# Running the value products of two key chunks one after the other, with seven score buffers

## The reference

```
q = (norm(x) @ wq.T + bq)      # 8 batches x 128 queries x 512
k = (ctx @ wk.T + bk)          # 8 batches x 2048 keys x 512
v = (ctx @ wv.T + bv)
scores = einsum('bhqd,bhkd->bhqk', q, k) / sqrt(32)      # 16 heads of 32
attn = softmax(scores)
out = einsum('bhqk,bhkd->bhqd', attn, v) @ wo.T + bo
```

## Time and profile before

| | |
|---|---|
| median of 3 runs | 1833.36 us (1832.06 to 1834.14) |
| the profiled execution, its own time | 1831.57 us |
| its span | 1829.8 us |
| granted TensorE clock, mean | 0.977 |
| TensorE busy | 1710.6 us, 93% of the span |
| VectorE busy | 1200.3 us, 66% |
| ScalarE busy | 962.1 us, 53% |
| GpSimd busy | 695.6 us, 38% |

### The profile page before, as it was taken

The page is one execution under the profiler, slowest core; times in us unless marked ns, Lnnn a source line. Parts: engine busy times, 40 slices in busy tenths (PEclk is TensorE's granted clock), DMA queues, the critical chain, the costliest instruction groups (busy, mean ns, idle before and its releaser), DMA issues. The chain is left out here.

```text
span 1829.8 us, 37829 instructions
## 1 busy us (share of the span) xinstructions
PE 1710.6 (93%) x15768; PEld 1376.8 (75%) x15768; DVE 1200.3 (66%) x1631; ACT 962.1 (53%) x1470; POOL 695.6 (38%) x315
## 2 busy tenths in 40 slices
PE   6899999999999999999999998567999689979999
PEld 5688888888888888888888887566887466658886
DVE  5126887878778778778778787767323677753223
ACT  2236666666666666666666666653210678730000
POOL 0003555555555555555555554002001466622220
PEclk9999999999999999999999999789999899999999
DMA  4211111111011011011110101042560533101101
GB/s 162 73 47 38 32 35 41 27 39 41 27 39 42 27 39 42 28 39 37 32 39 30 39 16 63 16 132 109 179 184 2 161 91 103 58 25 46 49 19 46
DMA packets 104192, 105.00 MB, mean 57 GB/s; under 512 B 7263, under 2 KB 72799, under 8 KB 104044
## 3 DMA queue, kind: packets, MB, share of 16 engines
q1 hardware_dynamic: 104044, 102.83, 18.5%
HBM read 79.74 MB, written 23.07 MB: 56 GB/s over the span
## 5 line engine op out<-in xcount | busy, mean ns | idle before, releaser
L528 POOL TENSOR_TENSOR b_acc<-b_acc,b_s 128x1024 f32<-128x1024 f32 x168 | 458.6, 2730 | 268.5 <-ACT b_s L731 258.1
L793 DVE TENSOR_TENSOR b_mx<-b_psS,b_mx 128x512 f32<-128x512 f32 x480 | 331.3, 690 | 50.0 <-PE b_psS L600 36.9
L760 DVE TENSOR_TENSOR b_s<-b_s,b_mb 128x2048 f32<-128x2048 f32 x128 | 350.9, 2743 | 15.7 <-ACT b_mb L718 15.7
L731 ACT ACTIVATE b_s<-b_s 128x2048 f32<-128x2048 f32 x128 | 245.1, 1915 | 67.1 <-DVE b_s L760 67.1
L740 ACT ACTIVATE b_s<-b_psS 128x2048 f32<-128x2048 f32 x128 | 241.1, 1883 | 56.3 <-DVE b_mx L793 55.9
L43 PE MATMUL b_work<-cT,wkT 128*128 128x512 f32 x512 | 210.7, 412 | 0.0
L43 PE MATMUL b_work<-wvT,cT 128*128 128x512 f32 x512 | 209.4, 409 | 0.0
L44 PE MATMUL b_work<-cT,wkT 128*128 128x512 f32 x512 | 200.8, 392 | 0.0
L45 PE MATMUL b_work<-cT,wkT 128*128 128x512 f32 x512 | 200.5, 392 | 0.0
L45 PE MATMUL b_work<-wvT,cT 128*128 128x512 f32 x512 | 200.2, 391 | 0.0
L44 PE MATMUL b_work<-wvT,cT 128*128 128x512 f32 x512 | 200.0, 391 | 0.0
(11 more groups left out here) (224 smaller groups left out, 3056.7 us busy)
## 6 DMA issues: line engine op xcount, KB each, us to landing
cin<-in_ctx SPq DMA_DIRECT2D x64, 512.0 KB, 3.7
q_scratch<-d_st SPq DMA_DIRECT2D x32, 256.0 KB, 2.5
k_scratch<-d_st SPq DMA_DIRECT2D x32, 256.0 KB, 2.5
e_q<-q_scratch SPq DMA_DIRECT2D x16, 512.0 KB, 3.5
k_sb<-k_scratch SPq DMA_DIRECT2D x64, 128.0 KB, 3.7
experts_sb<-in_L_ffn_expert_w SPq DMA_DIRECT2D x8, 1024.0 KB, 5.3
x_sb<-in_x SPq DMA_DIRECT2D x2, 1024.0 KB, 7.0
q_scratch<-a_q SPq DMA_DIRECT2D x4, 512.0 KB, 3.2
```

What stands on the lines that cost most here:

```text
L528: nc.gpsimd.tensor_tensor(acc[:, :, :], acc[:, :, :], s[:, buf, 2 * i:2 * i + 2, :], ALU.add).then_inc(sum_done, 1)
L731: nc.scalar.activation(part, part, ACT.Exp, scale=SCALE).then_inc(exp_done, 1)
L760: nc.vector.tensor_tensor(s[:, n % BUFS, :, :], s[:, n % BUFS, :, :], mb[:, :].rearrange("p (o n) -> p o n", o=1).broadcast_to([P, CHUNK, ...
L793: nc.vector.tensor_tensor(mx[:, :, :], part, mx[:, :, :], ALU.max).then_inc(mx_done, 1)
```

## The change

The value products of chunks 2k and 2k + 1 now stand in one beat, 34 + 4k, one right after the other. Chunks 0 and 1 stand in beat 2 of eight, chunks 2 and 3 in beat 6, both between T and S; beats 1 and 4 have none. There are seven score buffers in place of six (8 KB more of each partition).

```diff
-        BUFS = 6
+        BUFS = 7
...
-        def value_step(beat):
-
-            early, late = steps(beat, 32, 2, SLOTS * CHUNK), steps(beat, 33, 2, SLOTS * CHUNK)
-            if early is not None and early % CHUNK:
-                return early
-            return late if late is not None and late % CHUNK == 0 else None
+        def value_steps(beat):
+
+            n = steps(beat, 34, 4, SLOTS * CHUNK // 2)
+            return () if n is None else (2 * n, 2 * n + 1)
...
-                if (n := value_step(beat)) is not None:
+                for n in value_steps(beat):
                     outputs(n)
```

## The result

The changed kernel takes 1817.22 us (median of 6 runs, 1815.16 to 1820.62), the kernel before 1833.55 us in its six. The ratio is 0.9908, 95% interval 0.9895 to 0.9922: faster by 0.92%. Forecast were 1818.3 us, 14.5 us less. The medians differ by 16.3 us, and the interval of the ratio stands for 14.3 to 19.3 us. The profiled execution took 1817.25 us with a span of 1815.5, against 1831.57.

The account below looks back on a forecast made before the run. TensorE's instruction order bounds up to beat 255, a VectorE and ScalarE chain the tail. 0.47 us a slot over 28 slots, 13.0 us, plus 1.5 us tail, taken from 1832.8, gives 1818.3 us; 8-in-10 range 1813 to 1826.

Parts of the forecast that it names:

- Chunk 0: Projected region: its value product, alone between two projections, costs 1.20 us, appended 0.873; 0.33 us saved a slot.
- Chunk 2: Projected region: its value product between T and S costs 1.01 us, appended 0.873; 0.14 us saved a slot.
- The appended O: A value product right behind another costs 0.873 us, read from the tail; bounds 0.81 and 1.01 us.
- The prediction's sum by pauses alone: Projected region: two modes fewer entered and left a slot, about 0.2 us each over 28 slots, 11 us.
- The slack of 1.04 us: Between the end of chunk 3's move and S of chunk 0, 7.65 us after S of chunk 3; costed at nothing.
- the forecast break-even: Beat 4: the slot's 0.47 us gain is used up when the move ends over 8.12 us after its S starts.
- The rival: S of chunk 0, beat 4: the score move becomes the bound; at 8.6 us, about 1847 us; chance 0.04.
- The tail: After the projections, where S, maxima and move set the pace: 1.5 us gained, ends -4 and +2.
- The gain behind M: Tail: without O of chunk 2 the maxima start 1.06 us earlier, in two slots, 2.1 us.
- The loss before S of chunk 1: Tail: two pairs with denominators precede this S; they fit at full clock, but end near 3 us late at half clock.
- The rival by which joining saves little: Each O costs 1.01 us joined or not; 4 to 7 us gained with the tail, about 1827 us; chance 0.08.
- The rival by which the tail gives it back: Groups before S of chunk 1 run at half clock both times; 9 us left, about 1824 us; chance 0.12.

Follow-up runs that it names:

- the two partial changes: Against the kernel before, with seven buffers: only chunks 0 and 1 joined, 1823.40 us, ratio 0.9944; only chunks 2 and 3 joined, 1829.09 us, ratio 0.9971.
- the two groups: Tail stretches of profiles: old order of value products 90.43, 90.48, 92.94 us; pairs in the tail 88.80, 88.96, 89.45, 88.61, 89.26 us.

## Why the prediction was right

**What bounds.** TensorE's order set the time of the projected region before and after: the region shrank by what TensorE's own row of instructions lost, and repeats to 0.01 us when it is left alone.

**The terms.** Chunk 0: 0.33 us forecast, 0.36 measured by the experiment that moved it alone. Chunk 2: 0.14 forecast, 0.134 measured. Together 0.464 against 0.494 us a slot, 13.0 against 13.84 us. The missing 0.03 us is in the price of the lone O. The loads of two projections, from the second load behind S to T, first before and then in the changed kernel, where no O stands between them (the T of before is in the earlier trace rows):

```profile
616.85 0.19 PEld L44 LDWEIGHTS b_work<-cT,wkT 128*128 128x128 f32 x1
```

```profile
610.31 0.19 PEld L44 LDWEIGHTS b_work<-cT,wkT 128*128 128x128 f32 x1
...
612.60 0.19 PEld L45 LDWEIGHTS b_work<-cT,wkT 128*128 128x128 f32 x1
...
615.55 0.58 PEld L563 LDWEIGHTS b_work<-ident,cin 128*128 128x128 f32 x4
```

That is 623.32 - 616.85 = 6.47 us against 615.55 - 610.31 = 5.24: the O had cost 1.23 us, not 1.20. I had counted the steps behind the O as if they were the same without it. They take 0.229 us behind the O (eleven steps from 620.80 to 623.32) and 0.227 us deep in a run (thirteen from 612.60 to 615.55).

The appended O costs 0.87 to 0.88 us, as read from O and denominators in the tail; it was the term with the widest bounds and it held. The medians differ by 16.3 us and the two changed stretches of the profiles by 15.5; what is left is within what the unedited stages differ by.

**That it is the change of kind.** The transposes between the pair undo it all with the beats untouched, and the buffer alone is nothing. By the Trainium skill, TensorEngine Tiling (Array Packing), Key Properties, a change of tiling mode drains TensorE; the trace agrees, with 0.17 to 0.20 us before O behind T and before S, and 0.35 us before O behind a projection. Removing a pause did not give the whole of it back. Between T and S one pause of 0.20 us is gone with an O, and the appended O takes 0.07 us more than alone (0.88 for 0.81), since loads behind a pause start closer together: 0.13 us, and 0.134 was measured. The prediction's sum by pauses alone does not follow from its terms: a pause before O and one before S for each O taken out, 0.215 + 0.199 us, would be 23 us over 28 slots; 11 us counts one pause for each.

**What was costed at nothing.** The slack of 1.04 us in front of S of chunk 0 was there, and with two more maxima nearly all of it and of the time before the move was used at 0.06 us a slot. With three more the kernel became slower than before, at S-to-S 8.45 us; the forecast break-even was 8.12 us. The rival was real, and 1.5 us of VectorE work in each slot away from costing.

**The tail.** Forecast 1.5 us, with -4 and +2 as ends; 1.6 in the pair of profiles and 2.3 between the means of the two groups. The gain behind M came: the maxima start 1133.44 - 1129.38 = 4.06 us after M and 5.07 before, 1.01 us for the 1.06 forecast. The loss before S of chunk 1 came too: S comes 9.29 and 9.54 us after M in the two slots, where it was 9.99 and 9.92, and 8.98 both times in the order that puts one product alone in front of it. So the two slots of the forecast gave 0.70 + 0.38 = 1.1 us. The rest came from a place that the prediction put at nothing, the slot of the third M, which no S follows: from there to the output projection the changed kernel takes 23.09 us for 23.65. B comes there 2.43 us after M instead of 4.59, since O of chunk 2 no longer stands in front of it, but whether this gave the 0.56 us stays open: with the transposes between the pair, where the tail has the same order, this stretch took 23.66 us. That the forecast 1.5 us fits is in part luck, the more so as the clock moves a tail of the same order by 2.5 us.

The rival by which joining saves little is refuted by the two partial changes. The rival by which the tail gives it back did not come about.

## What to carry to other kernels

Where one engine is busy all the time with short groups of different shape, price a group by the start of what follows it, with and without it, and not by its duration or the pause alone: a group between two others of different kind cost 1.01 to 1.23 us here, appended to its like 0.87. Before such a move, find the shortest distance that it makes on the queue of another engine and compare it with the chain that must fit in; 1.04 us a slot was what made it free. Where that engine waits instead, the same groups fill its wait, and here their place in front of the waiting instruction was worth more than an early issue of it.

## What had not been expected of the hardware

The transposes behind a change of kind took 0.42 us from the first load to the end of the last, in a run 0.58 us. The maxima of VectorE with an extra semaphore step came at 0.76 to 0.77 us each instead of 0.72 (2.87 us for four). The scores that TensorE starts after 4.99 us of waiting, at two places in the tail of the changed kernel, run at half clock: 2.09 us for 1.17, with a granted clock of 0.50 from 1144.83 to 1146.92, where that of the S before it, at 1138.67, was 1.00. Lone loads behind a pause start closer together than the same loads in a run, so that 32 loads of O extend over 0.81 us alone and 0.88 us as the second half of a pair.
